# Moving the loop, value, query and key products of a two-layer graph network from the front stage into the mixing stage

## The reference

```python
W = jnp.einsum('rb,bio->rio', comp, basis)          # 8 relations from 4 bases
H = jnp.einsum('ni,rio->nro', x, W)
agg = jax.ops.segment_sum(H[src, etypes], dst, num_segments=N_NODES)   # 42500 edges
gnn = agg + x @ loop_weight + bias_param

qkv = (x @ Wqkv.T + bqkv)                           # 8 heads of 32
qn, kn = normalize(q) * (scale * temperature), normalize(k) * scale
kv_mod = jnp.einsum('bhni,bhnj,bhne->bhije', kn, kn, vN)
y = A * einsum(qn, qn, kv_mod) + scale**2 * einsum(qn, kv) + scale**4 * vsum
mix = (y[1:] / y[0]) @ Wproj.T + bproj
x = x + gnn + mix                                   # x inside gnn and mix is layernorm(x)
```

## Time and profile before

| | |
|---|---|
| median of 3 runs | 2142.92 us (2133.72 to 2148.55) |
| profiled execution | 2157.94 us, its span 2156.2 us |
| front, to the first matmul of the table stage | 0 to 104.1 us |
| table stage, to its last matmul | 104.1 to 353.6 us |
| turn to the mixing stage | 353.6 to 360 us |
| mixing stage and gather | 360 to 816 us |
| all the rest | 816 to 2156.2 us |

### The profile page before, as it was taken

One profiled execution on the slowest core, in us unless ns is written; L12 is line 12 of the kernel. 1 busy time (PEld: TensorE's weight loads), 2 busy tenths in 40 slices (PEclk: granted clock), 3 DMA queues, 4 the chain that ended last, 5 costly groups with the idle time before them and its releaser, 6 DMA issues. The chain is left out here.

```text
span 2156.2 us, 29667 instructions
## 1 busy us (share of the span) xinstructions
PE 1926.4 (89%) x8898; PEld 1248.8 (58%) x8898; DVE 1331.6 (62%) x2880; ACT 782.9 (36%) x2025; POOL 1028.3 (48%) x1084
## 2 busy tenths in 40 slices
PE   7988987879899888599976989999999899999999
PEld 3444544434344446499843766767678655656565
DVE  7688877878777875432275888888897612121221
ACT  4411123324232413144345555655542332333222
POOL 5678642777777770333185777777763300000000
PEclk9998999999989998699987999999999999999999
DMA  4178875777777771622156888877863000000000
GB/s 139 28 140 162 189 204 199 209 205 209 205 209 208 202 211 56 232 74 70 53 170 192 238 257 233 230 227 222 237 192 120 1 0 10 0 10 10 0 11 9
DMA packets 136148, 300.34 MB, mean 139 GB/s; under 512 B 27935, under 2 KB 72102, under 8 KB 135862
## 3 DMA queue, kind: packets, MB, share of 16 engines
q0 software_dynamic: 64432, 197.83, 32.3%
q1 hardware_dynamic: 71558, 100.61, 16.9%
HBM read 236.58 MB, written 61.64 MB: 138 GB/s over the span
## 5 line engine op out<-in xcount | busy, mean ns | idle before, releaser
L966 POOL DMA_INDIRECT rows<-h_table,row_rel x352 | 340.5, 967 | 155.1 <-issue 103.0
L2291 POOL DMA_INDIRECT rows_g<-g_table,row_src x352 | 335.1, 952 | 136.2 <-issue 103.0
L2654 PE MATMUL p_ag<-rows_g,oh_g 128*128 128x260 f32 x1408 | 364.4, 406 | 36.7 <-DVE rows_g L2405 29.3
L2654 PEld LDWEIGHTS p_ag<-rows_g,oh_g 128*128 128x128 f32 x1408 | 251.4, 195 | 117.4 <-issue 64.8
L3021 DVE SCALAR_TENSOR_TENSOR x<-p_yf,cw_f,x 128x256 f32<-128x256 f32 (+1 forms) x160 | 66.4, 478 | 279.6 <-PE p_yf L3181 279.6
L2405 DVE TENSOR_TENSOR rows_g<-rows_g,p_e 128x2048 f32<-128x2048 f32 x88 | 200.5, 2279 | 0.4 <-ACT p_e L2507 0.4
L408 POOL DMA_INDIRECT slot_table<-rec_f,dst_i x120 | 154.9, 1291 | 55.2 <-issue 55.2
L1091 DVE TENSOR_TENSOR fT<-a_sb,p_sel 128x512 f32<-128x512 f32 x200 | 128.0, 682 | 37.3 <-PE p_sel L1351 37.2
L3181 PE MATMUL p_yf<-f,h_f 128*128 128x256 f32 (+1 forms) x640 | 147.1, 383 | 0.8 <-ACT h_f L3073 0.8
L3131 PE MATMUL p_1f<-qT,f 128*128 128x512 f32 (+1 forms) x320 | 143.0, 590 | 0.5 <-ACT qT L3049 0.5
L3152 PE MATMUL p_2f<-h_f,f 128*128 128x512 f32 (+1 forms) x320 | 140.7, 582 | 0.4 <-DVEq L2968 0.4
(11 more groups left out here) (519 smaller groups left out, 3538.8 us busy)
## 6 DMA issues: line engine op xcount, KB each, us to landing
h_table<-h_out SPq DMA_DIRECT2D x80, 512.0 KB, 7.0
where_g<-d_table SPq DMA_DIRECT2D x88, 128.0 KB, 4.4
w<-in_L_ffn_W SPq DMA_DIRECT2D x16, 512.0 KB, 9.5
y_table<-yb_g SPq DMA_DIRECT2D x47, 128.0 KB, 1.7
rows<-h_table,row_rel POOLq DMA_INDIRECT x352, 3.7
rows_g<-g_table,row_src POOLq DMA_INDIRECT x352, 4.3
g_table<-row SPq DMA_DIRECT2D x20, 260.0 KB, 2.1
f<-in_L_ffn_W SPq DMA_DIRECT2D x16, 256.0 KB, 6.7
```

The lines of the kernel that those rows point to most:

```text
L966: pool.indirect_dma_start(rows[:, r, j].rearrange("p c d -> p (c d)"), None, st.h_rows, bass.IndirectOffsetOnAxis(ap=st.row_rel[:, at:at + ...
L2291: pool.indirect_dma_start(rows[:, r, j], None, st.g_table, bass.IndirectOffsetOnAxis(ap=st.row_src[:, at:at + 1], axis=0)).then_inc(gather ...
L2654: last = pe.matmul(p_a[:, k % NS, h, 0:HALF], oh[:, r, j], rows[:, r, j, h * HALF:(h + 1) * HALF], start=j % w == 0, stop=j % w == w - 1)
```

## The change

The products of loop, value, query and key leave the front. The front now only normalizes, transposes and stores xT; ACT does centre and scale in one instruction with a new column `lift`; the relation weights are begun by ACT (first base of all 8), DVE adds the other three bases of 5 relations, POOL those of the last 3. The edge records: PC is 12 instead of 11, so records(t) has 12 columns and 100 scatters are left instead of 120. In the table stage the two `squares` are gone and PE's order is turned: products(t + 1) stand ahead of records(t). The mixing stage begins with `dense(t)` for 20 tiles, which load xT back (4 buffers) and the weights (1 MB), with 13 batches of the gather among them; the key steps keep 3 batches a pair (and one at a pair's seam), the query blocks 3 each.

```diff
-PC = 11
+PC = 12
@@ table stage, PE
-            for t in range(T):
-                u = t % 2
+            def products(t):
                 pe.wait_ge(xT_in[t % XR], 16 * (t // XR + 1))
-                for q in range(4):
+                for q in range(HQ):
                     if t:
-                        pe.wait_ge(h_rest, 4 * (t - 1) + q + 1)
+                        pe.wait_ge(h_rest, HQ * (t - 1) + q + 1)
+                    else:
+                        pe.wait_ge(w_rel_first, min(2 * q + 2, REL_DVE))
+                        if 2 * q + 2 > REL_DVE:
+                            pe.wait_ge(w_rel_last, 2 * q + 2 - REL_DVE)
...
+            def records(t):
+                u = t % 2
                 pe.wait_ge(hot_ready, t + 1)
...
                 last.then_inc(hot_used, 1)
...
+            products(0)
+            for t in range(T):
+                if t + 1 < T:
+                    products(t + 1)
+                records(t)
@@ front, DVE
             dve.wait_ge(basis_in, 16 * (NB + 2))
-            dve.wait_ge(b_in, 32)
+            for r in range(REL_EARLY):
+                relation(r)
...
-                if t % 2:
-                    relation(t - 1)
-                    relation(t)
@@ front, POOL
+            for r in range(REL_DVE, R):
+                out = st.w_rel[:, :, r * D:(r + 1) * D]
+                for b in range(1, NB):
...
+                    pool.tensor_scalar(w_part[:, :, :], basis[:, b], comp[:, r * NB + b:r * NB + b + 1], None, ALU.mult).then_inc(w_step, 1)
...
+                    pool.tensor_tensor(out, out, w_part[:, :, :], ALU.add).then_inc(w_step, 1)
@@ mixing stage, tables of the order
-        AT_KV = [(1, 2, 3, 5, 6, 8, 9)] + [(SEAM, 1, 2, 4, 6, 7, 9)] * (PAIRS - 1)
+        AT_TILE = (2, 3, 5, 6, 7, 9, 10, 11, 13, 14, 15, 17, 18)
+        AT_KV = [(2, 5, 8)] + [(SEAM, 2, 5, 8)] * (PAIRS - 1)
@@ mixing stage, SP
+            load(0)
+            sp.dma_start(w_lv[:, :, 0:D], io["L0_gnn_loop_weight"].rearrange("(k p) o -> p k o", p=P)).then_inc(w_in, 16)
...
+            for t in range(XR, T):
+                sp.wait_ge(qk_ready, t - XR + 1)
+                load(t)
@@ mixing stage, DVE
+            def dense(t):
...
+                dve.tensor_tensor(x, x, p_sel[:, t % 2, 0:D], ALU.add).then_inc(loop_added, 1)
+                dve.tensor_tensor(v, p_sel[:, t % 2, D:].rearrange("p (h e) -> p h e", h=H),
+                                  b_v.rearrange("p (h e) -> p h e", h=H), ALU.add).then_inc(v_added, 1)
...
+                dve.tensor_tensor(part, p_qk[t % 2][:, :].rearrange("p (g e) -> p g e", g=2 * H),
+                                  b_qk.rearrange("p (g e) -> p g e", g=2 * H), ALU.add).then_inc(qk_used, 1)
...
+                link(dve.tensor_tensor(sq_t, part, part, ALU.mult))
+                link(dve.tensor_reduce(nrm3[:, :, t:t + 1], sq_t, AX, ALU.add))
@@ mixing stage, PE
+            for t in range(T):
+                dense(t)
+                if t in AT_TILE:
+                    sums(AT_TILE.index(t))
+            pe.wait_ge(qk_used, T)
```

More of the change, by code:

```diff
@@ L555, in _ @@
             dve.sem_inc(idx_ready, 1)
[L556 to L564 removed]
+            for r in range(REL_EARLY, REL_DVE):
+                relation(r)
             dve.wait_ge(mapped, 1)
@@ L648, in _ @@
                 if t == SQ_AT + 4:
+                    scales()
                     mixing_constants()
[L650 to L652 removed]
                 if t == 3:
@@ new lines, in _ @@
+            deviation(0, GT, 1)
+            normed(0)
+            for t in range(T):
+                if t + 1 == GT:
+                    turned(t)
+                    act.wait_ge(basis_in, 16 * (NB + 2))
+                    for r in range(R):
+                        nc.scalar.activation(st.w_rel[:, :, r * D:(r + 1) * D], basis[:, 0], ACT.Copy,
+                                             scale=comp[:, r * NB:r * NB + 1]).then_inc(w_begun, 1)
+                    deviation(GT, T, 2)
+                if t + 1 < T:
+                    normed(t + 1)
+                if t + 1 != GT:
+                    turned(t)
@@ L1125, in _ @@
             link(dve.memset(kx[:, :, :, :, FL - 1:], 1.0))
+            dve.sem_inc(one_made, 1)
+            for s in range(HOT_AHEAD):
+                one_hot(s)
+            dve.wait_ge(w_in, 80)
+            for t in range(T):
+                dense(t)
+                loops = t + 1
+                if t in AT_TILE:
+                    s = AT_TILE.index(t)
+                    sums(s, tiles_of(s))
+                    groups = GROUP[s]
+            lengths()
+            factors()
             for p in range(PAIRS):
@@ L1371, in turn_y, with dense @@
                 last.then_inc(y_turned, 1)
+            def dense(t):
+                pe.wait_ge(xT_in[t % XR], 16 * (t // XR + 1))
+                if t == 0:
+                    pe.wait_ge(w_in, 80)
+                for ready, used, out, w in ((lv_ready, lv_used, p_sel[:, t % 2], w_lv), (qk_ready, qk_used, p_qk[t % 2][:, :], w_qk)):
+                    if t >= 2:
+                        pe.wait_ge(used, t - 1)
+                    for k in range(K):
+                        last = pe.matmul(out, xT[:, t % XR, k * P:(k + 1) * P], w[:, k], start=k == 0, stop=k == K - 1)
+                    last.then_inc(ready, 1)
+            for t in range(T):
+                dense(t)
+                if t in AT_TILE:
+                    sums(AT_TILE.index(t))
+            pe.wait_ge(qk_used, T)
             for p in range(PAIRS):
```

332 lines of the change are left out of this document (134 added, 198 removed).

## The result

The changed kernel takes 2340.24 us (median of 4 runs, 2336.60 to 2345.64), the kernel before 2140.97 us beside it (4 runs, 2133.72 to 2148.55). The ratio is 1.093, 95% interval 1.089 to 1.098: 199 us slower. The prediction had the sign and the mechanism; 2340 lies above its 2274 and above its range of 2205 to 2310.

A forecast was written before the change was run, and what follows sets the result against it. PE was taken to bound the front and POOL's gather the mixing stage. Front -42, table stage +138 and mixing stage +36 gave +132 us, 2290 on the profiled execution, 2275 at the median; forecast 2274 us, range 2205 to 2310.

The forecast's parts named there:

- Rivals (2): Table stage: hots and low part hide beside products, tiles run at PE's 10.4 us, total 2069 us; chance 0.05.
- (3): Table stage: clock stays at the lower level through the whole burst, products 13.7 us, total 2415 us; chance 0.05.
- rival (1): Mixing stage: it stays on POOL's gather pace, 446 us, about 36 off, total 2239 us; chance 0.14.
- The table stage: From products(1) to the last record: a serial chain of 19.7 us a tile, 371 us instead of 233, 138 lost.
- The basis: Old table stage taken as 233 us; +132 on the profiled 2158 gave 2290, less 15 for the median, 2275.
- The front: Before the table stage: products of tile 1 start at 78 us, 42 earlier, with DVE's own chain late next.
- 20 maxima at 0.66: DVE in the front: the 20 maxima take 0.66 us each, 13.2 us.
- The term for POOL beside DVE: In the front: 2 us added for DVE instructions slowed beside POOL's; the exclusive lock would make it 7.7.
- The index steps: DVE in the front: the index steps take 3.0 us.
- The mixing stage ahead of the keys: Start of the mixing stage: 10 us of loads, 83 to 86 of products and sums, 7 of norms and first step; 100 us.
- The pairs: Mixing stage after the first keys: a pair takes 97 us, 4 pairs 388 us.
- Key step 2.53 us, 32 us a phase: Key phases of the mixing stage: 10 steps of 2.53 us with 3 or 4 sums and the seam, 32 us.

The follow-up runs named there:

- experiment 1: The changed kernel with PE's order in the table stage put back, a tile's products ahead of its own records: 2174.74 us, ratio 1.015.
- experiment 2: The changed kernel with PE's turned order kept, but DVE making the low parts of tile t-1 ahead of the hots of tile t: 2177.14 us, ratio 1.018.
- experiment 3: The kernel before with the turned order alone, products of tile t+1 ahead of records of tile t: 2288.32 us, ratio 1.068.
- run 6: The kernel of experiment 1 with the gathers of all but the first four batches left out, sums taking old rows: 2179.69 us.
- run 5: The changed kernel with 40 zero matmuls on PE behind the records of tiles 2 to 18, where PE waits: 2307.01 us, ratio 1.079.
- run 7: The kernel before with the gathers of all but the first four batches left out, sums taking old rows: 2114.34 us.
- run 9: The kernel of experiment 1 with all eight relations' sums on DVE and none on POOL: 2170.38 us, ratio 1.013.
- run 11: The kernel of experiment 1 with all transposes of the front put ahead of the 20 puts: 2170.97 us.
- run 4: The changed kernel with 36 zero matmuls on PE between the products of tile t+1 and the records of tile t: 2426.64 us, ratio 1.134.

## Why the prediction was right and wrong

**The mechanism was right.** Products, records, hots and low part are one chain in the changed kernel; experiments 1, 2 and 3 cut it, mend it and make it. Rivals (2) and (3) fell with the trace (a tile takes 18.5 to 20.4 us, the products 9.4 of it and not 13.7), rival (1) with run 6.

**The table stage, term for term.** Predicted 371 us from products(1) to the last record, 369.5 measured; hots 6.0, records 3.79 and low part with step 0.82, measured 5.96 (201.30 to 207.26), 3.78 (197.52 to 201.30) and 0.82; products with their clock loss 6.87 + 2.5 = 9.4, measured 8.4 to 9.9 and 9.37 in the mean, and run 5 puts 2.4 us a tile on the idle stretches. The rule that I cited from the Trainium skill (TensorE: Matmul & The Clock Gate, "HAM oscillation — how this bites in real kernels"), cold at every burst, holds here: every burst lost.

**What was wrong are four sizes, all to the same side.** Together they make some 69 us; the table stage, 2 us shorter than predicted, and roundings leave the 66 us between 2274 and 2340. The largest is the pairs of the mixing stage.

- *The basis, 19 us.* I took the 233 us of the old table stage from one profiled execution, added +138 to it and then took 15 us off for the median. Those us lay in that very stage: run 7 shows it 20 us shorter. Against run 7's the chain costs 157 us, and the profiled execution of the changed kernel lies 4 us below its median, not 15 above.
- *The front, 10 us.* 87.85 us, not 78. "20 maxima at 0.66" was the size that failed: they came at 1.16, 21.8 us from 42.99 to 64.78 where I had 13.2, since the puts ran at 1.2 GHz. I had taken DVE's duration from a stretch in which PE, with the moved products in it, ran at 2.4 GHz. The term for POOL beside DVE was mis-sized too: 2 us, where the six sums lost 7.18 - 4.80 = 2.4 and the three small instructions ahead 1.7 (2.63 us in the changed kernel, 0.97 in run 9's), 4.1 in all. By the Trainium skill's exclusive lock (SBUF — State Buffer, "SBUF: two separate sides") I had worked out 7.7 us for the six sums; the measured 2.4 decides, and the 4.1 for the whole lies between my 2 and those 7.7. The index steps, 1.7 us instead of 3.0, gave 1.3 back.
- *The mixing stage ahead of the keys, 7.5 us.* From its start to the first key features 107.5 us (571.32 - 463.8) instead of 100: load wait 10.4 where I had 10, the products with 13 sums 88 instead of 83 to 86, and 9.3 us of norms and first step instead of 7:

```profile
474.19 3.75 PE L1372 MATMUL p_sel<-kf 128*128 128x512 f32 x4 [16.15 <-DMA kf<-in_L_mix_bqkv]
...
567.83 2.15 DVE L963 RECIPROCAL nrm<-nrm 128x320 f32<-128x320 f32 x1
...
571.32 2.29 DVE L1025 TENSOR_TENSOR kf<-kx,p_sel 128x2048 f32<-128x2048 f32 x1 [0.28 <-ACT p_sel L1179]
```

- *The pairs, 32 us.* Predicted were 388 us, measured 420 (571.32 to 991.1), 12 of the 32 in the key phases and 19 in the query blocks. "Key step 2.53 us, 32 us a phase" held for pairs 2 to 4 (32.2, 32.9, 32.9) and not for the first, 42.5 us (571.32 to 613.84), which has the first queries and the memsets on DVE beside it; the kernel before shows the same 42 us there (361.30 to 403.47), and I took my row from its third pair. "Query block 13.04 us" was one of the shorter: within a pair the blocks of the kernel before are 11.8 to 19.3 us apart (L1337), and those of the changed kernel came to 14.0 in the mean (70.8, 72.2, 68.7 and 67.7 us for five). Run 6 shows that this is PE's and DVE's own pace, not a gather that fell behind, and in run 7, the kernel before without that pace, the blocks take 13.8 us in the mean.

The gather that paces the kernel before hid 24 us of the 99 that the moved work costs the mixing stage. "POOL is no longer the bound" was right; I had the growth at 36 us, and it was 75 (456 to 531 us).

**The account, from stage to stage.** Experiment 1 against run 7's front: gather 39.6 us earlier (340.1 to 300.5), mixing stage 72.7 us longer (455.2 to 527.9): 33 us slower. The medians say 2174.74 - 2140.97 = 33.8, and 31.8 against the kernel before that ran beside experiment 1. The turned order adds 165.5. Even with its order mended the change loses, since it moves 69 us of matmuls from a front, where they are worth 32 us, into a stage with 24 us of slack.

## What to carry to other kernels

When an instruction moves ahead of another on one engine, write down what the engine on the other side has queued in front of the thing that it now waits for; here one loop had to be turned on both engines or on neither (2177, 2175 and, on one alone, 2340 us). Price slack by taking the pacing thing away, as runs 6 and 7 did, before moving work beside it: a stage paced by a gather at 456 us had only 24 us to give. Take a duration for a sum from all its instances, not from one clean one, and ask whether the work that is moved away was what kept the neighbour fast.

## What the runs showed of the hardware that was not expected

- With fp16 matmuls of 340 columns (125 or 52 rows of input) whose rows left no gap for 18.8 us, each with a weight load of 0.18 us, PE stayed at a granted clock of 0.50 (run 11); in the kernel before, with f32 matmuls of 512 columns among them, it was 1.00.
- Zero matmuls in an idle stretch of 6.4 to 6.9 us brought the f32 products behind them from 9.4 us in the mean to 6.94 (run 5). Put ahead of the records instead, with the idle stretch left open, they brought them to 8.6 only (run 4).
- A DVE cast of 52x340 took 1.32 us beside POOL's sums and 0.33 without them, and a DVE sum with two SBUF inputs 1.20 and 0.80.
- The median time in which a store of 512 KB landed was 8.6 us in one execution and 6.5 in another of the same table stage; in the kernel before and its variants with the old order it was 5.5 to 8.6 us with 120 small scatters in the stage, 7.4 with 140, and 5.1 and 6.7 with 100.
